# A wait on ScalarE moved from the start of the adjacency build to its third turn, and two small DMAs moved ahead of the scatters

## The chip, the core and the metric

The kernel runs on one core of one Trainium2 chip. The core has TensorE for matrix products, VectorE, ScalarE and GpSimd for work on rows, SyncE that only issues DMAs, and 16 DMA engines that all of them share. In the profile TensorE is PE (PEld its weight loads), VectorE is DVE, ScalarE is ACT, GpSimd is POOL, SyncE is SP. The metric is the device time of one launch in microseconds, smaller being better.

## The reference, cut to what matters

3125 nodes with 256 features, 53,125 edges. Six steps of a gated graph network, then one mixture of experts with the best 2 of 8 for each node.

```python
def _L0_gnn_ref(node_feats, ..., src, dst):
    for _ in range(NUM_STEPS):                                   # 6
        h = jnp.maximum(node_feats @ W1.T + b1, 0.0) @ W2.T + b2
        msg = jax.ops.segment_sum(h[src], dst, num_segments=n_nodes)
        gx = msg @ W_ih.T + b_ih
        gh = node_feats @ W_hh.T + b_hh
        xr, xz, xn = jnp.split(gx, 3, axis=-1)
        hr, hz, hn = jnp.split(gh, 3, axis=-1)
        r = jax.nn.sigmoid(xr + hr)
        z = jax.nn.sigmoid(xz + hz)
        n = jnp.tanh(xn + r * hn)
        node_feats = (1.0 - z) * n + z * node_feats
    return node_feats

x = x + _L0_gnn_ref(_layernorm(x, axis=-1), ..., src, dst)
x = x + _L0_ffn_ref(_layernorm(x, axis=-1)[None], ...)[0]        # top 2 of 8 experts
```

## The kernel before

Each engine has an instruction list of its own, written out by hand, and the lists meet only at semaphores. The run has four parts.

**Preparation (0 to about 105 us).** Edges, weights and node features are loaded. The features, normalised, become the state in two half precision parts, `x_hi` and `x_lo`. VectorE's last write of `x_lo` raises `state_lo`. At that point SyncE (L402 to L404) stores both parts to DRAM, `x_kept`, 1.6 MB each, with the semaphore `x_kept` (16 for each). They are read back only on a slow path that these inputs don't take. From 23.7 us on two large DMAs from `fill_rows` also fill the slots of the experts in DRAM.

**Build (about 105 to 444 us).** The adjacency counts are built in 196 slices of 16 columns, in seven turns of 28. For slice `g` VectorE makes one-hot keys (`hots(g)`, L852), TensorE multiplies them into one of two banks (`slice_sums(g)`, L1551), ScalarE evicts the bank to `stage` (`evict(g)`, L1204) and GpSimd copies `stage` into `adj` (L499). There are RING = 2 banks, so slice `g + 2` can't be summed before slice `g` is evicted. The keys have DEEP = 4 sets, so `hots(g)` waits for the sums of slice `g - 4` or `g - 3`. On every engine's list a second piece of work goes `beside` the slices. In the first turn it is the first step's hidden layer: `relu_sum` on TensorE (L1486, L1491), `relu_hi` on ScalarE (L1171) and `relu_lo` on VectorE (L767), one in every three slices. In turn two it is the first window's messages. From the third turn on it is also the gates of the window before, and ScalarE's `state_hi` at slice 27 of that turn (L1197), which is the first instruction to overwrite a part of `x_hi`. VectorE's `state_lo` overwrites `x_lo` only after `state_hi`. ScalarE's list of the build begins with the wait that the change moves (L1225).

**Steps two to six (444 to about 1810 us).** Windows of 512 or 384 columns, `messages` (L1514) and `gate_sum` (L1538), nearly all of it on TensorE.

**Experts (about 1620 to 2043 us).** During the last step the finished windows are normalised and routed. GpSimd scatters each row with an indirect DMA to the slots of its two experts in DRAM (`scatter(w)`, L561), 50 DMAs in all, and those of the last window count on `scattered2`. SyncE, before it loads the first tile of slots (`load_tile`, L460), waits for all scatters to have landed. Each tile of 256 slots then goes through two layers on TensorE and is added to `out` by two indirect DMAs from GpSimd (L584). They count on `y_out0` and `y_out1`. VectorE's `output` (L1115) waits for `16 n + 16` on them before it overwrites the buffers of tile `n`, so both must hold 16 before the first tile. Two DMAs to the DRAM tensor `started` (L573) give this base count and have no other purpose. They stand behind the last scatter on GpSimd's queue.

Of the kernel before, what the change touches and what calls it, by code (L numbers as in the profile page):

```python
# [6 lines left out]
F32 = mybir.dt.float32  # L7
# [10 lines left out]
P = 128  # L18
# [20 lines left out]
GROUP = 28  # L39
# [34 lines left out]
NX = 8  # L74
# [3 lines left out]
TT = TILE // P  # L78
# [12 lines left out]
def gnn_ffn(nc, x, src, dst, W1, b1, W2, b2, W_ih, b_ih, W_hh, b_hh, Wg, bg, bias, F1, fb1, F2, fb2, out):  # L91
    stack = ExitStack()
    with stack:
        sems = {}

        def sem(name):
            if name not in sems:
                sems[name] = stack.enter_context(nc.semaphore(name))
            return sems[name]
# [155 lines left out]
        valid = lb("valid", [P, 1], F32)  # L255
        eid = lb("eid", [P, 4, NX], F32)
# [67 lines left out]
        slot_in = nc.dram_tensor("slot_in", (NX * CAP, ROW), F32, kind="Internal").ap()  # L324
        ffn_dram = nc.dram_tensor("ffn_scratch", (NX, P, 2, 2, DT * HID), F32, kind="Internal").ap()
        plane_dram = [nc.dram_tensor(f"plane_scratch{i}", (P, NT, ACOLS), F16, kind="Internal").ap() for i in range(2)]
        started = nc.dram_tensor("started", (TT, P), F32, kind="Internal").ap()
        x_kept = [nc.dram_tensor(f"x_kept{i}", (P, DT * NPAD), F16, kind="Internal").ap() for i in range(2)]
        bound_dram = nc.dram_tensor("bound_scratch", (2 * P, 2), I32, kind="Internal").ap()
        inputs = sem("inputs")  # L330
# [17 lines left out]
        def own(w):  # L348
            return w % 2 if w < NW - 1 else 2
# [123 lines left out]
        def _(pool):  # L473
# [76 lines left out]
            def scale(w):  # L550
                t0, nt = WIN_T0[w], WIN_TILES[w]
                pool.wait_ge(sem("var2"), w + 1)
                pool.tensor_tensor(rstd2[:, t0:t0 + nt], rstd2[:, t0:t0 + nt], expo2[:, t0:t0 + nt], ALU.pow).then_inc(sem("rstd2"), 1)

            def scatter(w):
                pool.wait_ge(sem("slot_of"), w + 1)
                pool.wait_ge(sem("diff_kept"), w + 1)
                for t in range(WIN_TILES[w]):
                    n = TAIL if WIN_T0[w] + t == NT - 1 else P
                    for k in range(2):  # L560
                        pool.indirect_dma_start(slot_in[:], bass.IndirectOffsetOnAxis(ap=slot_of[own(w)][0:n, k, t:t + 1], axis=0),  # L561
                                                x2_rows[own(w)][0:n, t, :], None).then_inc(sem(f"scattered{own(w)}"), 16)

            scale(0)
            for w in range(1, NW):
                scale(w)
# [2 lines left out]

            pool.wait_ge(sem("stored"), 16 * (NW + 1))  # L570
            pool.wait_ge(sem("tiles_of"), 1)
            for j in range(TT):
                pool.dma_start(started[j:j + 1, :].rearrange("a p -> p a"), valid[:], allow_slow_non_contiguous=True).then_inc(sem(f"y_out{j}"), 16)  # L573
            counts = [pool.value_load(tiles_of[0:1, e:e + 1], min_val=1, max_val=CAP // TILE) for e in range(NX)]
            done = pool.alloc_register("pool_tiles")
            pool.reg_mov(done, 0)
# [567 lines left out]
        def _(act):  # L1144
            a = nc.scalar
# [53 lines left out]
            def evict(g):  # L1199
                i, b = divmod(g, GROUP)  # L1200
                if b % 2 == 0 and g >= 4:
                    act.wait_ge(sem("stage_free"), g // 2 - 1)
                act.wait_ge(sem("slice_full"), g + 1)
                a.activation(stage[g // 2 % 2][:, :, (b % 2) * SW:(b % 2 + 1) * SW], bank[2 + (g + i) % RING][:, 0:NT * SW].rearrange("p (q c) -> p q c", c=SW),  # L1204
                             ACT.Copy, saturate=False, accum_out=over[:, g:g + 1]).then_inc(sem("stage_full"), 1)
                if b == GROUP - 1:
                    act.wait_ge(sem("deg_sum"), i + 1)
                    a.activation(degree[:, i * TURN_COLS:(i + 1) * TURN_COLS], bank[2 + (g + 1 + i) % RING][:, 0:TURN_COLS], ACT.Copy).then_inc(sem("deg_done"), 1)

            def beside(w, b):  # L1210
                if w == -1 and b % 3 == 1:
                    relu_hi(b // 3, b // 3, first=True)
                if w == 0 and b in (1, 3, 5, 7):
                    relu_hi(RELU_BUILD + b // 2, RELU_BUILD + b // 2, first=True)
                if w >= 0 and b == 15:
                    msg_hi(FIRST, w, 0)
                if w >= 0 and b == 26:
                    msg_hi(FIRST, w, 1)
                for f, places in enumerate(((4, 6, 9), (16, 18, 21))):
                    if w >= 1 and b in places:  # L1220
                        gate_act(FIRST, w - 1, f, places.index(b))
                if w >= 1 and b == 27:
                    state_hi(FIRST, w - 1)

            act.wait_ge(sem("x_kept"), 32)  # L1225
            for g in range(NSL):
                evict(g)
                beside(g // GROUP - 1, g % GROUP)
            gates(FIRST, NW - 2, 0)
# [593 lines left out]
```

## Time and profile before

| | us |
|---|---|
| median of the runs | 2048.14 (2046.22 to 2049.36, 3 runs) |
| the profiled execution | 2045.75 |
| its span, first to last instruction | 2043.7 |
| outside the span | 2.05 |
| PE busy | 1864.3 (91%) |
| DVE busy | 1104.2 (54%) |
| ACT busy | 575.3 (28%) |
| POOL busy | 335.9 (16%) |

The page's second part cuts the span in 40 slices of 51 us, each digit tenths busy:

```profile
PE   2769999999799999999999999999999999929996
DVE  6867888864144652444524445234452456635775
PEclk7789999999899999999999999999999999959998
DMA  8930000000443300000000000000000001463543
```

PE is full from the fourth slice to the 35th. Outside of that it has gaps in two places: up to about 130 us, and around slice 36, where the last step ends and the experts begin.

### The profile page before, as it was taken

To read this page: it belongs to the slowest core of one execution; us is meant where nothing else is said; L and a number is where in the kernel's file an instruction comes from. 1 tells how busy PE (TensorE), PEld (TensorE's weight loads), DVE (VectorE), ACT (ScalarE), POOL (GpSimd) and SP (SyncE) were. 2 spreads that over 40 slices of the span, in tenths; PEclk is the share of its full clock that TensorE was granted. 3 is DMA by queue.
4 is the path that set the end of the run, shared out by engine and by line. 5 is a ranking of instruction groups with operands and counts; after the bars stand their busy time and mean duration, and the time that the engine had idled before them with its cause. 6 is when DMAs were issued, how large, how long until landed. Compare 5 with 4: busy or idle time off the path is not lost.

```text
span 2043.7 us, 30436 instructions
## 1 busy us (share of the span) xinstructions
PE 1864.3 (91%) x10923; PEld 1118.3 (55%) x10924; DVE 1104.2 (54%) x2615; ACT 575.3 (28%) x1183; POOL 335.9 (16%) x454
## 2 busy tenths in 40 slices
PE   2769999999799999999999999999999999929996
PEld 2645555555344574445744457444574455629996
DVE  6867888864144652444524445234452456635775
ACT  0234444432021231122311223112231112216663
POOL 1011111100355500000000000000000013143665
PEclk7789999999899999999999999999999999959998
DMA  8930000000443300000000000000000001463543
GB/s 261 336 131 1 1 1 1 1 1 1 138 140 134 129 22 2 1 1 1 1 2 1 1 1 1 2 1 1 1 1 1 11 32 60 182 263 66 84 77 53
DMA packets 73943, 109.43 MB, mean 54 GB/s; under 512 B 11774, under 2 KB 64809, under 8 KB 72516
## 3 DMA queue, kind: packets, MB, share of 16 engines
q1 hardware_dynamic: 50526, 49.36, 7.7%
q0 software_dynamic: 18368, 38.09, 7.4%
q10 hardware_dynamic: 4902, 20.01, 2.4%
q8 instruction: 92, 1.51, 0.3%
q14 instruction: 55, 0.45, 0.1%
HBM read 43.59 MB, written 65.05 MB: 53 GB/s over the span
## 4 chain that ended last, share of the span: by engine, by line
PE 69%; issue 14%; POOL 6%; DVE 6%; ACT 2%; DMA 1%; POOLq 0%; SPq 0%; ACTq 0%; DVEq 0%
PE bank L1514 35%; PE bank L1538 24%; PE bank L1551 4%; PE bank L1491 4%; POOL out L584 3%; POOL slot_in L561 2%; POOL tick L583 1%; PE bank L1402 1%; DMA x_kept<-x_lo 1%; PE bank L1486 1%; DVE hot_key L852 1%; ACT stage L1204 1%; DVE r_lo L767 1%; DVE xa L723 0%; ACT m_hi L1177 0%
## 5 line engine op out<-in xcount | busy, mean ns | idle before, releaser
L1514 PE MATMUL bank<-adj,r_hi 128*128 128x512 fp8e4 (+4 forms) x2100 | 732.0, 352 | 0.0
L1514 PE MATMUL bank<-adj,r_lo 128*128 128x512 fp8e4 (+4 forms) x2100 | 732.0, 352 | 0.0
L1514 PEld LDWEIGHTS bank<-adj,r_hi 128*128 128x128 f16 x2100 | 205.7, 98 | 188.1 <-issue 1.4
L1514 PEld LDWEIGHTS bank<-adj,r_lo 128*128 128x128 f16 x2100 | 205.6, 98 | 188.1 <-issue 1.3
L774 DVE SCALAR_TENSOR_TENSOR m_lo<-bank,msg_unit,m_hi 128x512 f16<-128x512 f32 (+4 forms) x84 | 57.2, 682 | 280.9 <-ACT m_hi L1177 280.9
L1538 PE MATMUL bank<-x_hi,wht_hi 128*128 128x512 f16 (+4 forms) x504 | 177.4, 352 | 0.8 <-DVE m_lo L774 0.5
L1538 PE MATMUL bank<-m_hi,wct_hi 128*128 128x512 f16 (+4 forms) x504 | 177.3, 352 | 0.0
L1538 PE MATMUL bank<-m_lo,wct_hi 128*128 128x512 f16 (+4 forms) x504 | 177.3, 352 | 0.0
L1538 PE MATMUL bank<-m_hi,wct_lo 128*128 128x512 f16 (+4 forms) x504 | 177.3, 352 | 0.0
L1538 PE MATMUL bank<-x_lo,wht_hi 128*128 128x512 f16 (+4 forms) x504 | 177.3, 352 | 0.0
L1538 PE MATMUL bank<-x_hi,wht_lo 128*128 128x512 f16 (+4 forms) x504 | 177.3, 352 | 0.0
L852 DVE TENSOR_SCALAR hot_key<-iota_key,slot_key 128x400 f16<-128x400 f16 x588 | 156.3, 325 | 0.0
L1177 ACT ACTIVATE m_hi<-bank,msg_unit 128x512 f16<-128x512 f32 (+4 forms) x84 | 53.0, 632 | 350.8 <-PE bank L1514 344.8
L1551 PE MATMUL bank<-hot_key,hot_row 128*128 128x400 f16 x588 | 127.8, 336 | 24.5 <-ACT stage L1204 17.1
L1204 ACT ACTIVATE stage<-bank 128x400 fp8e4<-128x400 f32 x196 | 98.3, 503 | 170.3 <-PE bank L1551 149.8
L548 POOL MEMSET x_rows<- 128x4 f32 (+1 forms) x3 | 0.2, 97 | 836.7 <-PE bank L1713 836.7
L767 DVE SCALAR_TENSOR_TENSOR r_lo<-bank,r_hi 128x512 f16<-128x512 f32 (+1 forms) x78 | 51.2, 667 | 156.6 <-ACT r_hi L1171 155.6
L1184 ACT ACTIVATE gate_a<-gate_a,gate_bias,gate_unit 128x512 f32<-128x512 f32 (+4 forms) x84 | 63.8, 759 | 233.0 <-DVE gate_a L790 233.0
L793 DVE SCALAR_TENSOR_TENSOR gate_z<-degree,deg_w,bank 128x512 f32<-128x512 uint16 (+4 forms) x84 | 56.8, 676 | 97.7 <-PE bank L1538 97.6
L1188 ACT ACTIVATE gate_a<-gate_a,gate_bias,gate_unit 128x512 f32<-128x512 f32 (+4 forms) x84 | 63.6, 758 | 160.5 <-DVE gate_a L804 155.5
L499 POOL COPY adj<-stage 128x200 uint32<-128x200 uint32 x98 | 45.4, 463 | 337.3 <-ACT stage L1204 337.3
L1551 PEld LDWEIGHTS bank<-hot_key,hot_row 128*128 128x128 f16 x588 | 55.5, 98 | 77.2 <-ACT stage L1204 26.9
(288 smaller groups left out, 2918.5 us busy)
## 6 DMA issues: line engine op xcount, KB each, us to landing
slot_in<-fill_rows SPq DMA_DIRECT2D x2, 13520.0 KB, 68.7
ffn_scratch<-pair POOLq DMA_DIRECT2D x32, 512.0 KB, 3.2
ffn_w<-ffn_scratch ACTq DMA_DIRECT2D x8, 2048.0 KB, 16.1
x_rows<-in_L_ffn_W POOLq DMA_DIRECT2D x32, 256.0 KB, 3.9
slot_x<-slot_in SPq DMA_DIRECT2D x30, 260.0 KB, 3.3
xa<-in_x SPq DMA_DIRECT2D x1, 3072.0 KB
x<-in_x ACTq DMA_DIRECT2D x1, 3072.0 KB
out<-x SPq DMA_DIRECT2D x4, 512.0 KB
```

The lines of the kernel that those rows point to most:

```text
L584: pool.indirect_dma_start(out[:], bass.IndirectOffsetOnAxis(ap=dest[j][:, 0:1], axis=0), slot_y[j][:], None, bounds_check=N - 1, oob_is_er ...
L767: v.scalar_tensor_tensor(r_lo[:, 2 * u:2 * u + m, :].rearrange("p t d -> p (t d)"), bank[4 + u % 4 if first else 2 + u % 2][:, 0:m * D], 0 ...
L774: v.scalar_tensor_tensor(m_lo[:, w % 2, f, 0:n], bank[f][:, 0:n], msg_unit[:, 0:1], m_hi[:, w % 2, f, 0:n], ALU.mult, ALU.subtract)\
L793: ins = v.scalar_tensor_tensor(z, dg, deg_w[:, 2 + f:3 + f], bank[5][:, 0:n], ALU.mult, ALU.add)
L852: last = v.tensor_scalar(hot_key[k][:], iota_key[:], slot_key[:, g, s:s + 1], None, ALU.is_equal)
L1184: a.activation(gate_a[:, 0:n], gate_a[:, 0:n], ACT.Sigmoid, bias=gate_bias[:, f:f + 1], scale=gate_unit[:, f:f + 1]).then_inc(acts, 1)
L1188: a.activation(gate_a[:, 0:n], gate_a[:, 0:n], ACT.Tanh, bias=gate_bias[:, 4 + f:5 + f], scale=gate_unit[:, 4 + f:5 + f]).then_inc(acts, 1)
L1204: a.activation(stage[g // 2 % 2][:, :, (b % 2) * SW:(b % 2 + 1) * SW], bank[2 + (g + i) % RING][:, 0:NT * SW].rearrange("p (q c) -> p q c" ...
L1491: last = mm(o[:, k * D:(k + 1) * D], xs[:, t, n0:n0 + P], ws[:, t, :], start=False, stop=True, skip_group_check=True)
L1514: last = mm(bank[f][:, 0:n], r[:, q, f * P:(f + 1) * P], c, start=q == 0 and i == 0, stop=q == NT - 1 and i == len(todo) - 1)
L1538: last = mm(bank[b][:, 0:n], wgt, mov, start=i == 0, stop=i == len(todo) - 1)
L1551: last = mm(bank[2 + (g + i) % RING][:, 0:NT * SW], hot_row[b // 2 % 2][:, b % 2, s, :], hot_key[k][:], start=s == 0, stop=s == SLOTS - 1)
```

## The change

ScalarE no longer waits for `x_kept` ahead of slice 0 but ahead of slice 56, the first of the third turn. The two DMAs to `started` are issued ahead of the first `scale` on GpSimd, thus before the first scatter. Each now copies eight numbers of one partition, 32 bytes in one piece, where each copied one number of 4 bytes from each of 128 partitions. SyncE's list, which issues the store, is unchanged.

```diff
-        started = nc.dram_tensor("started", (TT, P), F32, kind="Internal").ap()
+        started = nc.dram_tensor("started", (TT, NX), F32, kind="Internal").ap()
@@
+            for j in range(TT):
+                pool.dma_start(started[j:j + 1, :], eid[0:1, 0, :]).then_inc(sem(f"y_out{j}"), 16)
             scale(0)
             for w in range(1, NW):
                 scale(w)
@@
             pool.wait_ge(sem("stored"), 16 * (NW + 1))
             pool.wait_ge(sem("tiles_of"), 1)
-            for j in range(TT):
-                pool.dma_start(started[j:j + 1, :].rearrange("a p -> p a"), valid[:], allow_slow_non_contiguous=True).then_inc(sem(f"y_out{j}"), 16)
@@
-            act.wait_ge(sem("x_kept"), 32)
             for g in range(NSL):
+                if g == 2 * GROUP:
+                    act.wait_ge(sem("x_kept"), 32)
                 evict(g)
                 beside(g // GROUP - 1, g % GROUP)
```

## Rows read from the trace of the kernel before

**Rows 1.** The page, part 4: the chain that ended last, by engine

```profile
PE 69%; issue 14%; POOL 6%; DVE 6%; ACT 2%; DMA 1%; POOLq 0%; SPq 0%; ACTq 0%; DVEq 0%
```

**Rows 2.** Timeline of ACT: start, duration, instruction, idle time before it and its releaser

```profile
123.47 0.50 ACT L1204 ACTIVATE stage<-bank 128x400 fp8e4<-128x400 f32 x1 [18.32 <-DMA x_kept<-x_lo]
...
129.68 0.59 ACT L1171 ACTIVATE r_hi<-bank 128x512 f16<-128x512 f32 x1
```

**Rows 3.** Timeline of SP, same columns, where it issues the store

```profile
105.38 2.52 SPq L404 DMA_DIRECT2D x_kept<-x_hi  x1
107.94 0.46 SPq L404 DMA_DIRECT2D x_kept<-x_lo  x1
```

**Rows 4.** Timeline of PE, the first sums of the build

```profile
107.42 1.16 PE L1551 MATMUL bank<-hot_key,hot_row 128*128 128x400 f16 x3 [2.80 <-DVE hot_key L852]
...
111.02 0.67 PE L1551 MATMUL bank<-hot_key,hot_row 128*128 128x400 f16 x3
124.12 2.18 PE L1551 MATMUL bank<-hot_key,hot_row 128*128 128x400 f16 x6 [12.43 <-ACT stage L1204]
```

**Rows 5.** Timeline of DVE over the same stretch

```profile
112.20 0.78 DVE L852 TENSOR_SCALAR hot_key<-iota_key,slot_key 128x400 f16<-128x400 f16 x3
125.07 0.69 DVE L767 SCALAR_TENSOR_TENSOR r_lo<-bank,r_hi 128x512 f16<-128x512 f32 x1 [12.08 <-ACT r_hi L1171]
...
130.30 0.69 DVE L767 SCALAR_TENSOR_TENSOR r_lo<-bank,r_hi 128x512 f16<-128x512 f32 x1 [1.88 <-ACT r_hi L1171]
```

**Rows 6.** By stretch: busy us of PE, PEld, DVE, ACT, POOL, granted clock, DMA share, GB/s

```profile
107.40:110.60 3.20, 3.18 (x14) 1.98 (x15) 2.44 (x10) 0.00 (x0) 0.00 (x0) 0.50 1.09 336
110.60:114.00 3.40, 1.09 (x8) 0.55 (x6) 1.26 (x4) 0.00 (x0) 0.00 (x0) 0.99 1.11 399
...
124.00:127.70 3.70, 3.58 (x14) 2.05 (x15) 2.63 (x9) 2.23 (x8) 0.73 (x2) 0.50 0.00 1
...
131.10:154.70 23.60, 21.36 (x153) 13.97 (x151) 23.57 (x78) 13.33 (x45) 4.33 (x10) 1.00 0.01 1
154.70:179.00 24.30, 23.22 (x147) 13.98 (x146) 20.26 (x65) 12.02 (x40) 4.18 (x8) 1.00 0.01 2
```

**Rows 7.** Line 1197: count, duration ns min/median/max, first and last start

```profile
L1197 ACT ACTIVATE x_hi<-x_new x35: 719/967/1057, 248.8 to 1536.2; 128x1024 f16<-128x1024 f32 x16, 128x768 f16<-128x768 f32 x8, 128x896 f16<-128x896 f32 x6, 128x620 f16<-128x620 f32 x4
```

**Rows 8.** Timeline of POOL, the end of the scatters and the first output

```profile
1821.91 1.55 POOL L561 DMA_INDIRECT slot_in<-x_rows,slot_of  x1 [0.30 <-issue]
1823.47 1.21 POOL L573 DMA_DIRECT2D started<-valid  x2
1858.66 0.29 POOL L583 TENSOR_TENSOR tick<-valid 128x1 f32<-128x1 f32 x1 [33.99 <-DVE slot_y L1117]
```

**Rows 9.** Timeline of POOL, the first `scale` (the two DMAs' new place)

```profile
1611.86 1.05 POOL L553 TENSOR_TENSOR rstd<-rstd,expo 128x4 f32<-128x4 f32 x1 [54.05 <-DVE rstd L1007]
```

**Rows 10.** Timeline of SP, the loads of the first tiles

```profile
1833.51 45.81 SPq L460 DMA_DIRECT2D slot_x<-slot_in  x8
```

**Rows 11.** Timeline of PE at the first tile

```profile
1836.52 1.09 PE L1752 MATMUL bank<-ident,slot_x 128*128 128x128 f32 x4 [14.46 <-DMA slot_x<-slot_in]
```

**Rows 12.** The page: queue q14 (part 3), DMA issues with us to landing (part 6)

```profile
q14 instruction: 55, 0.45, 0.1%
...
out<-slot_y,dest POOLq DMA_INDIRECT x58, 3.8
...
started<-valid POOLq DMA_DIRECT2D x2, 0.5 KB, 9.3
```

**Rows 13.** DMA queues, 1826 to 1828 us: packets, MB, share of 16 engines

```profile
q0 software_dynamic: 16, 0.02, 16.9%
q14 instruction: 1, 0.01, 7.0%
```

**Rows 14.** DMA queue q0, 1768 to 1770 us, behind another window's last scatter

```profile
q0 software_dynamic: 17, 0.00, 0.9%
```

**Rows 15.** Busy time by stretch while SyncE waits, columns as in Rows 6

```profile
1828.00:1830.00 2.00, 0.00 (x0) 0.00 (x0) 0.00 (x0) 0.00 (x0) 0.00 (x0) 0.50 0.00 0
```

## The prediction

> **What bounds the kernel now.** I read the page first, then the timelines of the places that the edit touches. By the chain that ended last, 69% of the span is TensorE and only 1% a DMA [rows 1]. So only time on the chain counts, and a wait of ScalarE matters where TensorE or VectorE stand behind it. It does at the start of the build. ScalarE's first eviction starts at 123.47 after 18.32 us of idle time, ended by the landing of the store of `x_lo` [rows 2]. SyncE issued that store at 105.38 to 108.40, when the state was complete [rows 3]. TensorE had summed slice 0 by 108.58 and slice 1 by 111.69, has only two banks, and stands for 12.43 us until 124.12 [rows 4]. VectorE has filled its four sets of keys and slice 4's by 112.98, then idles 12.08 us [rows 5]. Nothing else runs on the core. All three engines are waiting for a copy that only the slow path reads.
>
> The second place is the end of the scatters. The last one is issued at 1821.91, the two DMAs to `started` at 1823.47 [rows 8], but SyncE's first load of a tile goes out only at 1833.51 [rows 10]. TensorE stands 14.46 us for that load [rows 11].
>
> **Edit 1, the wait of ScalarE.** It removes no work. What is gained is the time for which the engine that sets the pace stood still. In the first turn that is VectorE: between 131.1 and 154.7 it is busy for 23.57 of 23.60 us, TensorE for 21.36, ScalarE for 13.33 [rows 6]. So I count VectorE's idle time. It is 12.08 us ahead of the first `relu_lo` and 1.88 us ahead of the second [rows 5], together 13.96.
>
> Is the first really gone? Without the wait ScalarE evicts slice 0 at about 108.7 and slice 1 at 111.8, each 0.5 us with a read of 0.2 behind it, and `r_hi` (0.59, [rows 2]) ends at about 113.0. VectorE is free at 112.98, so its first `relu_lo` moves from 125.07 to 113.0. The second pause came because TensorE restarted at half of its clock: 0.50 granted from 124.0 to 127.7, after 12.43 us without a matmul [rows 4, 6]. In the new order the clock has already risen at 110.6, after 3.18 us of work in 3.20 [rows 6], and TensorE goes on. It then needs about 0.5 us for each of slices 2, 3 and 4 and 1.6 for the hidden sums between, with 0.4 of waiting for the eviction of slice 1: slice 4 is summed at about 115.1, evicted by 115.8, and `r_hi` ends at about 116.4. VectorE, busy for 3.35 us between its two pauses (125.07 to 128.42), arrives at 116.33. The second `relu_lo` moves from 130.30 to 116.4, thus by 13.9. From there on the engines meet the same work in the same state. I take **14.0 us**. The lower bound is 12.1, if the second pause stays, less about 1 for one more stretch of 3.4 us at half clock. The upper bound is 123.47 less 108.7, 14.8.
>
> The moved wait costs nothing. The copies have landed at 123.4. Turns two and three share the 94 us from 154.7 to 248.8 [rows 6, 7], so the third begins near 200 today and near 186 then, and what queues behind the wait on ScalarE, eviction 56 and with it banks and keys, isn't held. The first overwrite of `x_hi` is at 248.8 [rows 7]. The cover is over 60 us. The evictions now run beside the store. VectorE and TensorE ran beside the DMAs at 336 GB/s and more from 107.4 to 114.0 [rows 6], and VectorE's three keys took the 0.78 us [rows 5] of any later set, so I cost that at nothing. From the second turn TensorE is the fullest engine (23.22 of 24.30, [rows 6]), and everything later hangs on semaphores, not on a time, so the 14 us should reach the end.
>
> **Edit 2, the two DMAs.** In their new place they are two issues of 0.60 us on GpSimd's queue. GpSimd is idle there for 54.05 us, ended by VectorE's statistics [rows 9], so 1.2 us are hidden. If they weren't, the first `scale` would be 1.2 us late, with a scatter behind it and TensorE full beside both. In the old place their own landing covers nothing: GpSimd then waits 33.99 us for the first output [rows 8], and VectorE needs the base count only ahead of that, over 20 us after 1833. By the waits alone this edit is worth 0.
>
> The queue says more. These two DMAs of 512 bytes took 9.3 us to land, where an indirect DMA of 128 rows takes 3.8 [rows 12]. They wrote 256 pieces of 4 bytes. The last scatter needed until shortly before 1833.51, which is 11.6 us from its issue. From 1826 to 1828 q0 has only 16 packets, but they hold 16.9% of 16 engines in 2 us, 5.4 us, and one instruction packet holds 7.0%, 2.2 us [rows 13]. Over the run 55 such packets take 0.1% of the engines' span, about 0.6 us each [rows 12]. From 1828 to 1830 nothing moves [rows 15]. Behind the last scatter of another window q0's last 17 packets hold 0.9%, and its tail is over at once [rows 14]. So something on one or a few engines stands, just while the 4 byte writes are landing (1824.1 plus 9.3 is 1833.4), and the last rows of the scatter stand with it. My reading is that these writes are the cause. With them gone the 16 packets of 1826 to 1828 end by 1828, and half a microsecond for landing and issue puts the load at 1828.5: **5.0 us**. Bounds are 0 (the stall belongs to the scatter itself) and, if the last scatter lands in 3.8 us, 1833.5 less 1825.7, 7.8. Below nothing I see no reason for, since nothing is added there.
>
> One rule speaks against this gain. The Trainium skill, in DMA: Bandwidth & Descriptors, section Queues, rings and completion order, says that a completion increment lands only after the earlier writes of its DMA engine. The two DMAs are issued behind the scatter. By that rule alone they can't hold its increments, the 5.0 would be 0 and the sum 14.0. No row here shows which write stood first on an engine. The same page, section Specifications, has writes under 512 bytes done as a read and a write, which fits 9.3 us for 512 bytes but names no effect on others.
>
> **The sum.** The profiled execution took 2045.75, with 2.05 outside its span: 2045.75 less 14.0 less 5.0 is 2026.75. It lies 2.4 below the median of the runs, so against 2048.14 the forecast is **2029.1**.
>
> **The rivals.** (A) Both edits pay, 2029.1, its own range 2026 to 2031.5. (B) Only the first pays, since the stall at 1826 has another cause, the scatter's own last pieces or the instruction packet: 2048.1 less 14.0, 2034.1, own range 2032.5 to 2036. For it stands that the stall ends in the scatter's queue, against it the 9.3 us. (C) The first pays but gives a part back, for instance VectorE meets ScalarE or GpSimd in another phase in the first turn: 8 to 11 us less, 2037 to 2040. The 23.57 of 23.60 speaks against. (D) It does nothing: another wait ends as late as the store. ScalarE's list has none, 2048. (E) Slower, through TensorE's clock. In the profile the clock rose for good, at 127.7, only behind the pause. If it stayed at 0.50 through the first turn, TensorE's 21.36 us in the stretch of 23.6 would become up to 42.7, so 19.1 are lost in it. That overtakes the 14 us from some 31 us at half clock on (14 of 19.1, times 42.7). For the whole turn, 1.3 such stretches, it would be 2048.1 less 14 plus 25, 2059. Against it stands the clock of 0.99 already from 110.6 to 114.0 on the same work [rows 6].
>
> **How the numbers follow.** A 0.52, B 0.36, C 0.06, D 0.03, E 0.03. A is the likeliest, so 2029.1. A and B hold 0.88, so the range is theirs, 2026 to 2036. 0.2%, about 4.1 us, is what a measurement of this kernel can tell from no change. A, B and C are faster by more: 0.94. D is the same, E slower.
>
> **What would show it.** ScalarE's first eviction at about 108.7 and no wait for `x_kept` in the list of waits; TensorE's pause at 111.7 under 1 us; a granted clock of 1.00 from 110.6 on; `relu_lo` at 113.0 and 116.4; the first `x_hi` at 234.8. For edit 2: no queue packet over 1 us behind the last scatter, and the first tile's load about 6.5 us behind the last scatter's issue instead of 11.6. If that distance stays, B is right. If `relu_lo` is on time but the build's last slice isn't 14 us early, C is.

## The result and the profile after

| | before | changed |
|---|---|---|
| median of the runs, us | 2047.93 (2046.22 to 2049.36, 4 runs) | 2024.63 (2022.20 to 2026.74, 4 runs) |
| ratio | | 0.9886, 95% interval 0.9869 to 0.9903 |
| the profiled execution | 2045.75, span 2043.7 | 2026.74, span 2024.7 |

The change makes the kernel 23.3 us faster in this measurement. 2029.1 was forecast, and the range of 2026 to 2036 misses the median by 1.4 us. The two profiled executions are only 19.0 us apart, which is the sum that was forecast. Measured again twice, the difference was 20.8 and 20.9 us, so some 2.5 us of the 23.3 did not come again.

Below are the lines of the changed kernel that answer to the rows of before. In this program TensorE's lines have numbers one higher.

ScalarE's timeline at the start of the build (start, duration, instruction, idle time before it and its releaser), for [rows 2]:

```profile
107.56 0.50 ACT L1204 ACTIVATE stage<-bank 128x400 fp8e4<-128x400 f32 x1 [3.47 <-PE bank L1552]
...
114.49 0.59 ACT L1171 ACTIVATE r_hi<-bank 128x512 f16<-128x512 f32 x1
```

TensorE's, for [rows 4]. Behind slice 0 at 106.36 the slices go on without the 12.43 us pause:

```profile
106.36 1.16 PE L1552 MATMUL bank<-hot_key,hot_row 128*128 128x400 f16 x3 [2.81 <-DVE hot_key L852]
...
109.82 1.18 PE L1552 MATMUL bank<-hot_key,hot_row 128*128 128x400 f16 x6
...
111.18 0.68 PE L1552 MATMUL bank<-hot_key,hot_row 128*128 128x400 f16 x3 [0.18 <-ACT stage L1204]
```

VectorE's, for [rows 5]. Neither `relu_lo` has idle time before it:

```profile
111.82 0.68 DVE L767 SCALAR_TENSOR_TENSOR r_lo<-bank,r_hi 128x512 f16<-128x512 f32 x1
...
115.13 0.68 DVE L767 SCALAR_TENSOR_TENSOR r_lo<-bank,r_hi 128x512 f16<-128x512 f32 x1
```

Busy time by stretch, columns as in [rows 6]. The granted clock is 1.00 from 109.3 on and stays there through the build:

```profile
105.90:109.30 3.40, 2.94 (x13) 1.87 (x14) 2.88 (x12) 0.59 (x2) 0.00 (x0) 0.50 1.07 329
109.30:112.70 3.40, 3.22 (x25) 2.16 (x24) 2.17 (x7) 2.05 (x7) 0.41 (x2) 1.00 1.12 384
112.70:116.00 3.30, 3.05 (x24) 2.02 (x22) 3.30 (x12) 2.00 (x7) 0.66 (x2) 1.00 1.02 430
```

GpSimd's timeline, for [rows 8] and [rows 9]. The two DMAs stand ahead of the first `scale` and hide in its idle time, and nothing is issued behind the last scatter at 1807.67:

```profile
1543.89 1.09 POOL L565 DMA_DIRECT2D started<-eid  x2 [0.36 <-issue]
1597.57 1.05 POOL L553 TENSOR_TENSOR rstd<-rstd,expo 128x4 f32<-128x4 f32 x1 [52.60 <-DVE rstd L1007]
...
1807.67 1.55 POOL L561 DMA_INDIRECT slot_in<-x_rows,slot_of  x1 [0.30 <-issue]
```

SyncE's first load, and TensorE's first instruction on it, for [rows 10, 11]:

```profile
1814.81 21.62 SPq L460 DMA_DIRECT2D slot_x<-slot_in  x4
```

```profile
1817.84 1.09 PE L1753 MATMUL bank<-ident,slot_x 128*128 128x128 f32 x4 [9.81 <-DMA slot_x<-slot_in]
```

The DMA queues from 1813 to 1815, 5.3 to 7.3 us behind the last scatter's issue (packets, MB, share of 16 engines). In [rows 13] the instruction packet held 7.0% of such a stretch, here it holds 1.7%:

```profile
q0 software_dynamic: 6, 0.02, 2.4%
q14 instruction: 1, 0.01, 1.7%
```

The 19.0 us between the two spans come apart as follows, each from the starts above. From slice 0 to the second `relu_lo` the kernel before takes 22.88 us, the changed one 8.77: 14.1 less. From the last scatter's issue to TensorE's first instruction on a tile it is 14.61 and 10.17: 4.4 less. The preparation happened to be 1.1 us shorter (slice 0 at 106.36, not 107.42), the long middle, from the second `relu_lo` to the last scatter's issue, 0.9 longer (1691.6 and 1692.5), the experts 0.3 shorter.

### The profile page after: what moved, and what is told of

Read it like the earlier page. It is cut to its first block, busy times and chain, and to the rows that moved or that the text cites. A ratio compares the mean times of both kernels' runs of the same rounds, so it can differ in the third digit from the quotient of the medians.

```text
span 2024.7 us, 30435 instructions
## 1 busy us (share of the span) xinstructions
PE 1861.4 (92%) x10923; PEld 1116.8 (55%) x10924; DVE 1103.0 (54%) x2615; ACT 575.3 (28%) x1183; POOL 337.7 (17%) x454
## 4 chain that ended last, share of the span: by engine, by line
PE 69%; issue 14%; DVE 7%; POOL 6%; ACT 2%; DMA 1%; POOLq 0%; SPq 0%; ACTq 0%; DVEq 0%
PE bank L1515 35%; PE bank L1539 24%; PE bank L1552 4%; PE bank L1492 4%; POOL out L584 3%; POOL slot_in L561 2%; POOL tick L583 1%; DVE hot_key L852 1%; PE bank L1487 1%; DVE r_lo L767 1%; ACT stage L1204 1%; DMA out<-slot_y,dest 1%; DVE st L668 0%; DVE xa L723 0%; ACT m_hi L1177 0%
## 5 line engine op out<-in xcount | busy, mean ns | idle before, releaser
L1515 PEld LDWEIGHTS bank<-adj,r_lo 128*128 128x128 f16 x2100 | 205.7, 98 | 188.2 <-issue 1.3
L1515 PEld LDWEIGHTS bank<-adj,r_hi 128*128 128x128 f16 x2100 | 205.7, 98 | 188.0 <-issue 1.4
L584 POOL DMA_INDIRECT out<-slot_y,dest x58 | 90.6, 1563 | 20.4 <-issue 12.4
```

What stands on the lines that cost most here:

```text
L584: pool.indirect_dma_start(out[:], bass.IndirectOffsetOnAxis(ap=dest[j][:, 0:1], axis=0), slot_y[j][:], None, bounds_check=N - 1, oob_is_er ...
L1515: last = mm(bank[f][:, 0:n], r[:, q, f * P:(f + 1) * P], c, start=q == 0 and i == 0, stop=q == NT - 1 and i == len(todo) - 1)
```

## The experiments

Theories: **S**, both edits pay, 14.0 and about 4.5 to 5 us, and the rest of the 23.3 is scatter of the runs. **W** and **Q**, one of the edits is worth more outside of the profile. **N**, the stall behind the last scatter has nothing to do with the two DMAs. Ratios are against runs of the kernel before on the same chip. "Behind" is the time from the last scatter's issue to the first tile's load: 11.6 us before, 7.1 in the changed kernel.

### Each edit alone, and both again

The first kernel takes only the last part of the diff, that of ScalarE, the second only the parts of the two DMAs, the third is the changed kernel. The fourth is the kernel before with the 256 small pieces kept and only the place changed:

```diff
+            for j in range(TT):
+                pool.dma_start(started[j:j + 1, :].rearrange("a p -> p a"), valid[:], allow_slow_non_contiguous=True).then_inc(sem(f"y_out{j}"), 16)
             scale(0)
```

> Only ScalarE's wait is moved; the two DMAs to started stay late and in 256 pieces of 4 bytes. Theory S (both parts pay, 14.0 and 4.5 us as the trace of the changed kernel shows them, and the rest of the measured 23.3 us is scatter of the runs): 14 us faster than before, and the first tile's load again about 11.6 us behind the last scatter's issue. Theory W (the wait is worth more outside the profile than in it): 17 to 19 us faster. Theory Q (the late DMAs cost more outside the profile): 14 us here.

> Only the two DMAs to started are early and in one piece; ScalarE waits for the store before the build. Theory S: 4.5 us faster, load 7.1 us behind the last scatter's issue. Theory W: 4.5. Theory Q: 7 to 9 us faster. Theory N (the stall behind the last scatter has nothing to do with these DMAs, its absence from one trace is chance): 0, and a load 11 to 12 us behind the last scatter's issue.

> The changed kernel again, on the same chip as its parts. Theory S: 18.5 to 19 us faster than before, the sum of the parts. Theories W and Q: 23 us, with the excess in one of the parts.

> The kernel before with the two DMAs to started moved ahead of the first scale, still 256 pieces of 4 bytes. If the place is what counts (nothing slow behind the last scatter): as much as a2, 4.5 us, since at 1557 us nobody waits for their 9 us. If the form is what counts: 0 to 1 us less than that would show, because nobody waits there either, so this run tells place plus form from form only together with the next one, late in one piece. Theory N: 0.

| | median us | less than before (2045.31) | ratio, interval | behind, us |
|---|---|---|---|---|
| the wait alone | 2031.66 | 13.7 | 0.9934, 0.9919 to 0.9949 | 11.4 |
| the DMAs alone | 2039.59 | 5.7 | 0.9974, 0.9964 to 0.9985 | 6.7 |
| both | 2024.49 | 20.8 | 0.9897, 0.9879 to 0.9914 | 6.6 |
| DMAs early, 256 pieces | 2038.58 | 6.7 | 0.9968, 0.9958 to 0.9979 | 6.9 |

The parts sum to 19.4 of 20.8. The wait is worth its 14 us, so W falls: 13.7 from the kernel before, 15.1 with the DMAs already moved (2039.59 less 2024.49). The DMAs are worth 5.7 us when moved in the kernel before, 6.7 when moved and left in 256 pieces, and 7.2 when left late beside the moved wait (2031.66 less 2024.49). S expected 4.5 and 18.5 to 19 for both, Q 7 to 9 and 23. The intervals of the two kernels with the DMAs early (about 3 to 7 and 4 to 9 us) hold 4.5 as well as 7, so between S and Q these runs do not decide.

N falls, since the stall is there wherever the pieces are late and gone wherever they aren't. With the wait alone, GpSimd and SyncE show it like this:

```profile
1807.40 1.56 POOL L561 DMA_INDIRECT slot_in<-x_rows,slot_of  x1 [0.30 <-issue]
1808.96 1.21 POOL L573 DMA_DIRECT2D started<-valid  x2
```

```profile
1818.78 0.41 SPq L460 DMA_DIRECT2D slot_x<-slot_in  x1
```

And its DMA queues from 1812 to 1814, 4.6 to 6.6 us behind the issue. Eight packets hold 14.7% of 16 engines, 4.7 us, and the instruction packet again over 2 us:

```profile
q0 software_dynamic: 8, 0.01, 14.7%
q14 instruction: 1, 0.01, 7.2%
```

Nearly all of the 4.7 us belongs to a single packet. From 1812.3 to 1812.5 the scatter's queue has this one alone, and it holds 134.6% of 16 engines for 0.2 us, thus 4.3 us:

```profile
q0 software_dynamic: 1, 0.00, 134.6%
```

The kernel before has the same, one packet of 4.6 us. The instruction packet, which rival B had as a possible cause, is there in the changed kernel too and takes 0.5 us (1.7% of 16 engines' 2 us). So it is not the cause: where the packed pieces are not in flight, neither of the two packets stands.

### What it is about the late DMAs that costs

All four start from the changed kernel. The first brings the two DMAs back behind the last scatter, in one piece each. The second does it in 256 pieces whose addresses lie 1 KB apart. The third issues four DMAs of 128 pieces instead of two. The fourth leaves them early and changes the scatters of the last tile, which then take all 128 rows instead of 53, the 75 unused ones with a slot out of bounds. That this brings them from one engine to all 16 is a theory, which no view of the trace can show:

```diff
+                pool.dma_start(started[j:j + 1, :, 0:1].rearrange("a p c -> p (a c)"), valid[:], ...)   # second; started is (TT, P, 256)
...
-                    n = TAIL if WIN_T0[w] + t == NT - 1 else P                                          # fourth
+                    limit = dict(bounds_check=NX * CAP - 1, oob_is_err=False) if last_tile else {}
-                        slot_of[own(w)][0:n, k, t:t + 1] ... x2_rows[own(w)][0:n, t, :]
+                        slot_of[own(w)][:, k, t:t + 1] ... x2_rows[own(w)][:, t, :], None, **limit
```

> The changed kernel with the two DMAs to started back behind the last scatter, but each still in one piece of 32 bytes. Theory F (the 256 small pieces make the stall): as the changed kernel, 2024 to 2025 us, load about 6.7 us behind the last scatter's issue, no DMA packet over 1 us there. Theory P (anything issued behind the last scatter on GpSimd's queue holds it up): as a1, 2031 to 2032, load 11 to 12 us behind.

> The changed kernel with the two DMAs late and in 256 pieces of 4 bytes, as before, but each piece goes to an address 1 KB from the next instead of 4 bytes. Theory F1 (the pieces wait for one another because they fall in the same few memory lines): as the changed kernel, 2024 to 2026, load 7 to 8 us behind the last scatter's issue. Theory F2 (a small piece is slow wherever it goes): as a1, 2031 to 2032, load 11 to 12 us behind.

> The changed kernel with four late DMAs of 128 pieces of 4 bytes in place of two; the two more count on a semaphore that is waited for only at the end. Theory F: the stall grows with the pieces, from 4.5 us over the changed kernel to 8 or 9, load 15 to 16 us behind the last scatter's issue, 2035 to 2037 us. Theory P or a fixed price of a late DMA: as a1, 11 to 12 us behind, 2031 to 2032.

> The changed kernel, whose load still goes out 6.7 us behind the last scatter's issue, where earlier windows' scatters land 2.4 us after theirs. The last tile's two scatters take all 128 rows instead of 53, the 75 unused rows with a slot out of bounds that the DMA skips; VectorE gets one small operation more. Theory K (53 rows go to one DMA engine, 128 to all 16): issue 0.96 us instead of 1.57, landing within 3 us of the issue, load about 4 us earlier, 2020 to 2021 us. Rival (the tail is slow because the scatter is the last and memory is still busy with the weights): no gain, 2024 to 2025.

| | median us (before: 2048.18) | ratio, interval | behind, us |
|---|---|---|---|
| one piece, late | 2026.58 | 0.9892, 0.9875 to 0.9908 | 7.2 |
| 256 pieces 1 KB apart, late | 2026.66 | 0.9897, 0.9880 to 0.9913 | 6.9 |
| 512 pieces, late | 2033.60 | 0.9927, 0.9910 to 0.9943 | 12.5 |
| last tile in 128 rows | 2023.76 | 0.9884, 0.9867 to 0.9900 | 3.3 |

So neither the place alone nor the small size alone does it. Late in one piece costs nothing, and late in small pieces that lie apart costs nothing either. The cost needs both late and packed pieces. My expectation for the doubled pieces was wrong: one microsecond more, not four. In time, too, the 512 pieces cost 7.0 us beside the kernel with one piece late, no more than the 7.2 that 256 cost above.

The last kernel tells the other half. In its trace the last scatter has landed 2.4 us behind its issue, and the load goes out 3.3 us behind. So the changed kernel's 6.6 to 7.1 us hold about 3.5 that the form of the last tile's scatters costs. The time fell less than I expected, to 2023.76 and not to 2020 to 2021.

### TensorE's clock and the store

The first kernel is the kernel before with TensorE kept busy in its pause. The second is the changed kernel without store and wait. The third and the fourth are the changed kernel and the one with the last tile in 128 rows, both again.

```diff
             for g in range(NSL):
+                if g == 2:
+                    for _ in range(54):
+                        mm(bank[0][:], ones_h[:], x_hi[:, 0, 0:512], start=True, stop=True)
                 slice_sums(g)
```

> The kernel before, in which TensorE fills its pause behind slice 1 with 54 matmuls on a bank that nobody reads, 11.5 us at the full clock. ScalarE's wait stays. My step for the second pause (TensorE restarts at half clock, so the second relu_lo comes 1.88 us late): clock 1.00 behind the pause, second relu_lo 3.4 us behind the first instead of 5.2, 1.9 us faster than before. Rival (the pause is the order of the first slices, not the clock): 5.2 us between them, no gain.

> The changed kernel without the store to x_kept and without the wait; it leaves out the copy that only the slow path reads, 3.2 MB of DMA. Theory S (store and evictions don't disturb each other): as the changed kernel, 2024.5, relu_lo at the same times. Theory W2 (the store beside the first turn costs something): 1 us or more faster.

> The changed kernel a third time. The ratio was 0.9886 and 0.9897. If the 23.3 us of the first measurement was mostly scatter of the kernel before: ratio 0.989 to 0.991, 19 to 22 us. If there is a gain of 4 us outside what the traces show: 0.988 to 0.989, 23 us again.

> The changed kernel with the last tile's scatters on all 128 rows, next to the changed kernel on the same chip. By the distance from the last scatter's issue to the load, 3.3 us against 6.7, less 1 us for the later issue: 2 to 3 us faster than the changed kernel.

| | median us (before: 2045.00) | ratio, interval |
|---|---|---|
| before, kept busy | 2043.85 | 0.9992, 0.9982 to 1.0001 |
| no store | 2026.45 | 0.9905, 0.9889 to 0.9922 |
| changed, again | 2024.08 | 0.9896, 0.9879 to 0.9912 |
| last tile in 128 rows, again | 2022.46 | 0.9891, 0.9875 to 0.9908 |

Kept busy, TensorE has the full clock behind the pause, and VectorE's second idle time is gone:

```profile
123.00:127.70 4.70, 4.51 (x30) 2.60 (x28) 2.97 (x10) 3.14 (x12) 0.73 (x2) 1.00 0.00 0
```

```profile
124.73 0.69 DVE L767 SCALAR_TENSOR_TENSOR r_lo<-bank,r_hi 128x512 f16<-128x512 f32 x1 [11.25 <-ACT r_hi L1171]
...
128.21 0.69 DVE L767 SCALAR_TENSOR_TENSOR r_lo<-bank,r_hi 128x512 f16<-128x512 f32 x1
```

The second `relu_lo` follows the first by 3.5 us instead of 5.2. The trace bears out 1.8 to 1.9 us as the price of the slow restart at that place. That they reach the end isn't shown: the timed runs give 1.1 us with an interval that holds no change, and in this trace the middle takes 1694.0 us, the longest of all 17. Taking the store out brings nothing: from slice 0 to the first `relu_lo` it is 5.7 us without it and 5.6 with it in the run beside it. Its median is 2.4 us higher, and its trace has that in the preparation and in the experts, not in the build. The kernel with the last tile in 128 rows has the lowest median both times, here by 1.6 us under the changed kernel, where I expected 2 to 3, and before by 2.8 under the one with one piece late. The 1.6 us are less than these runs can tell apart.

### How many pieces, how close, and what they hold up

The first kernel leaves one of the two late DMAs in 128 pieces. The second has the last tile's scatters in 128 rows and the 256 pieces late. The third puts 64 bytes between the pieces (`started` is (TT, P, 16)).

> The changed kernel with one late DMA of 128 pieces of 4 bytes and one late in one piece. Load behind the last scatter's issue so far: 6.7 us with no such pieces, 11.4 with 256, 12.5 with 512. If the stall saturates once there are pieces: 10 to 11.5 us, 2030. If it is proportional up to 256: 9 us, 2027.

> The last tile's scatters on all 128 rows, and the 256 pieces late again. Theory E (the pieces hold up only what is still queued behind them in time, the 53 rows on one engine): load 3.3 to 4 us behind the last scatter's issue, 2022 to 2023, the late pieces harmless. Rival (the pieces hold up every engine's last writes, as the two increments 5 us late in the traces suggest): 8 us or more behind, 2027 or more.

> 256 late pieces of 4 bytes, each 64 bytes from the next (4 bytes gave 11.4 us, 1 KB gave 6.9). If pieces wait for one another only inside one 64 byte line: 6.9 us, 2025 to 2026. If in a larger stretch: 8 to 11 us, 2028 to 2031.

| | median us (before: 2042.63) | ratio, interval | behind, us |
|---|---|---|---|
| 128 pieces, late | 2027.46 | 0.9929, 0.9913 to 0.9946 | 11.5 |
| last tile in 128 rows, 256 pieces late | 2028.48 | 0.9926, 0.9910 to 0.9943 | 2.8 |
| 256 pieces 64 bytes apart | 2025.21 | 0.9910, 0.9894 to 0.9927 | 6.9 |

64 bytes apart are enough, and 128 packed pieces cost as much time behind the scatter as 256 (ratio 0.9929, against 0.9934 with 256). The second kernel refutes the theory that was put for it. The load does go out early, 2.8 us behind, but then it runs into the stall itself. Its page entries, DMAs issued with their time to landing:

```profile
slot_x<-slot_in SPq DMA_DIRECT2D x1, 260.0 KB, 9.4
started<-valid POOLq DMA_DIRECT2D x1, 0.5 KB, 7.7
```

The same load without late pieces (last tile in 128 rows, again):

```profile
slot_x<-slot_in SPq DMA_DIRECT2D x1, 260.0 KB, 3.4
```

The load's queue, packets, MB and share of 16 engines, first beside the late pieces (1808 to 1818), then without (1809 to 1814):

```profile
q1 hardware_dynamic: 272, 0.27, 50.4%
```

```profile
q1 hardware_dynamic: 272, 0.27, 21.2%
```

The same 272 packets hold the engines for 81 us in all (50.4% of 160), not 17 (21.2% of 80). So 4 to 6 us are lost whether the scatter (4.4, its landing at 11.1 instead of 6.7) or the load (6.0) is in flight.

## Why the prediction was right and where it was wrong

**What bounds the kernel: right for the two places.** Both were the right ones, and no other stretch moved beyond what equal stretches differ by. But the account of before, with TensorE full from the fourth slice to the 35th and gaps in two places only, leaves one out. Between 509 and 527 us TensorE stands for 6.97 us until VectorE's `x_lo` is there and a little later for 6.29 more. The changed kernel has the same two pauses (6.97 and 6.40) 15 us earlier, untouched.

**Edit 1, 14.0 us: right.** 14.1 in the profile, 13.7 when done alone (the interval is about 10 to 17, so the runs can't tell 14.0 from the lower bound of 12.1). The two idle times are the sum, 12.08 and 1.88, and the experiment with the busy TensorE separates the second in the trace. I had `relu_lo` at 113.0 and 116.4, it came at 111.8 and 115.1, of which 1.1 us is the earlier slice 0. The first `x_hi` is overwritten at 233.7 (forecast 234.8), and no wait for the store is in the list of waits. The store beside the evictions costs nothing, as said. The start isn't the same in every execution: in two of the 13 traces without the wait at the start the clock rises 5.9 us behind the start of slice 0 and not 2.9 as in the changed kernel's first, and from there to the second `relu_lo` it takes 9.8 us, where the others take 8.8 to 9.0. That is the 1 us of my lower bound for one more stretch at half clock.

**Edit 2: place and mechanism right, the size right in the traces and open in the runs.** The stall comes from the 4 byte writes. I took 5.0 us for it. The first pair of traces shows 4.4. From the last scatter's issue to TensorE's first instruction on a tile the four other traces with 53 rows and packed late pieces take 13.9 to 15.3 us, the eight others without them 9.5 to 10.0. The timed runs give 5.7, 6.7 and 7.2, and the intervals of the first two hold 5.0.

The rule of the Trainium skill (DMA: Bandwidth & Descriptors, section Queues, rings and completion order) that spoke against the gain does not bound it here. With the pieces behind the scatter its last increment came 11.1 us after its issue, without them 6.7. By that rule an increment needs only its own engine's earlier writes. The trace doesn't contradict it: a packet of the scatter itself stood, for 4.3 and 4.6 us, while the packed small writes were under way. What doesn't hold is the step from the rule to a gain of 0.

**The stall's end, partly wrong.** I had its end at half a microsecond behind 1828, so 6.6 us behind the last issue, and that is what the changed kernel shows (7.1, later 6.6 and 6.7). But I took these 6.6 us for the end of the scatter's normal landing. They aren't: with 128 rows it lands in 2.4. That the 53 rows all go through one engine remains my reading of this.

**The rivals.** B, D and E fell. E's clock, which was to stay low, rose at 109.3 and stayed up through the build. C fell too: the build has its 14.1 us at the second `relu_lo`, and the middle, 0.9 us longer in the first pair, takes 1689.3 to 1693.1 us in the 13 traces without the wait at the start and 1691.6 to 1694.0 in the four with it, so nothing is given back there.

**The step that failed: the 2.4 us between the profiled execution and the median.** I added 2.4 us to the sum because the one profiled execution of before lay that much below its median, and I put a range around it that had no width for this. In the changed kernel the profiled execution lay 2.1 us above the median. So the term of +2.4 measured -2.1, and these 4.5 us are the whole distance from 2029.1 to 2024.6. The sum of the two edits, 19.0 us, came to 19.0 in the profiled executions and to 23.3, 20.8 and 20.9 in the runs: 2026.75 was forecast for the profiled execution and 2026.74 came. That this is exact is luck, since a shorter preparation (1.1) and expert part (0.3), a longer middle (0.9) and terms off by 0.1 and 0.6 happen to cancel.

My own upper bounds (14.8 and 7.8) gave 2025.5, and I stopped at 2026. 2024.63 lies below both. With the 20.8 or 20.9 us of the two repeats the median would have been about 2027 and in the range.

What varies can be seen. From TensorE's first instruction on a tile to the end of the span it took from 203.5 to 209.1 us in 17 traces, with nearly the same work in it. The kernel before and the one kept busy in its pause run the same instructions there and took 207.2 and 203.7. What separates them is mostly the clock. In the changed kernel's first profile it rises at 1826.2, TensorE is busy for only 0.80 of the next 3.4 us, and it falls back for 3.4 more:

```profile
1818.00:1826.20 8.20, 6.70 (x31) 6.30 (x31) 0.84 (x3) 2.30 (x6) 0.00 (x0) 0.50 0.12 34
1826.20:1829.60 3.40, 0.80 (x6) 0.57 (x5) 2.27 (x7) 2.09 (x7) 0.00 (x0) 1.00 0.00 0
1829.60:1833.00 3.40, 3.40 (x18) 3.40 (x17) 0.00 (x0) 0.95 (x2) 0.00 (x0) 0.50 0.30 78
```

In the repeat (changed, again) it rises at 1823.7, TensorE is busy for half of the next stretch, and it stays up:

```profile
1817.70:1823.70 6.00, 4.45 (x19) 4.08 (x20) 0.84 (x3) 1.50 (x4) 0.00 (x0) 0.50 0.15 47
1823.70:1827.00 3.30, 1.65 (x14) 1.41 (x13) 1.18 (x4) 2.60 (x9) 0.00 (x0) 1.00 0.00 1
```

The expert part took 206.9 us in the first and 204.0 in the second. At half clock TensorE was for 11.8 us of it in the first (8.4 and 3.4) and for 6.0 in the second. The 5.8 us more are worth at most 2.9 us of work, which is the difference. Of the 17 traces nine have the fall back, three of them for about twice as long, and take 205.7 to 209.1. Eight have none: six of them take 203.5 to 205.2, and the two with the last tile in 128 rows 205.7 and 205.8. The kernel before has one trace, with the fall. Whether its runs have it more often than those of the changed kernel, which would make the medians lie further apart than two like traces, isn't settled. It could also explain why the DMAs are worth 5.7 to 7.2 us in the runs and 4.4 in the trace, and isn't shown to.

**Open** is why 128 packed pieces stall as long as 256, and 512 only 1 us longer. That the stall reaches a packet of another write, an instruction packet and a load is shown, in what part of the chip it sits is not. Open too is why the first measurement gave 23.3 us and the repeats 20.8 and 20.9.

## What to carry to other kernels

A wait in front of a loop should stand where its data is first overwritten: here a copy that nobody reads in time stopped three engines, and the idle time of the engine that sets the pace gave the gain (13.96 us read, 14.1 in the profile, 13.7 in the runs). A DMA that only serves to raise a semaphore should be one contiguous piece or stand away from any transfer that someone waits for; here either was enough. And a forecast within 1% needs a width for what equal executions differ by, here about 3 us in the expert part alone, mostly from the clock, beside the bounds of its own terms. One profiled execution doesn't say where the median lies.

## What the runs showed of the hardware

- Behind 128 or 256 writes of 4 bytes to neighbouring addresses in DRAM one packet of the scatter in flight took 4.1 to 4.6 us (5.1 behind 512), and the longest in the changed kernel 0.6. 256 such writes 64 bytes or 1 KB apart did not do this (load 6.9 us behind the last scatter in both, 11.4 when packed). A load of 260 KB on another queue took 9.4 us beside them, not 3.4.
- An indirect scatter of 53 rows lands 6.2 to 6.7 us behind its issue and takes 1.55 us to issue. One of 128 rows, 75 of them out of bounds, takes 1.00 us and lands in 2.4.
- An instruction packet of 8 KB took over 2 us in the stall, where the run's mean is about 0.6 us and the one at the same place in the changed kernel took 0.5.
